# Attention by pairs of heads: both heads' output matmuls of a query quarter in one slot of the 20

## The chip, the cores and the metric

The kernel runs on one core of one Trainium2 chip. The metric is the device time of one execution in microseconds (us), and lower is better. Engine names are those of the profile: PE is the tensor engine's matmuls and PEld its weight loads, DVE is VectorE, ACT is ScalarE, POOL is GpSimd, and SP issues DMAs.

## The reference, cut to what matters

The network has three stages: a state-space convolution block, an attention block, and a mixture of eight experts. Only the attention is touched by the change.

```python
# x: (8, 128, 32, 32) float32 -> t: 8 images of 1024 tokens, 128 channels, 8 heads of 128
t = t + attn(ln(t))          # attention, below
t = t + experts(ln(t))       # router, top 2 of 8, gated experts

keys, queries, values = (einsum('btd,hod->bhto', x, W.reshape(8, 128, 128)) for W in (Wk, Wq, Wv))
dot  = einsum('bhqe,bhke->bhqk', queries, keys) / sqrt(128)
attn = softmax(where(causal, dot, -inf))
out  = einsum('bhqk,bhke->bqhe', attn, values).reshape(8, 1024, 1024)
return out @ Wu.T + bu
```

## The kernel before, in words

The attention takes the images in order and, in each, the eight heads as four **pairs**. There are 32 pairs `g`, four to an image (`g % 4` is 0 for an image's first pair and 3 for its last). The queries of a pair are cut into four **quarters** of 256 queries, and both heads of a quarter stand side by side in one matmul of 512 columns. A pair is worked off in 20 **slots**. The slot number `T` counts through all pairs, and `p = T % 20` is the slot within the pair. A slot handles one piece: the scores of one block of 128 keys against one quarter.

Each engine walks over the same slots `T` in its own instruction queue, in a fixed order written out in its loop, and waits on semaphores.

- **PE** issues, in slot `T`: three matmuls of `scores(T)` into one of three rotating PSUM banks, then the side work of the slot, then three matmuls of `attend(T - 3)` (the weighted sum, which needs the exponentials of three slots ago). `LAG = 3` is that distance. Scores and attend are done as three products of high and low halves (`mm3`, lines 1272 to 1274).
- **ACT** takes two exponentials of each piece (line 1439 writes `pf`, line 1441 the rounded `phi`), and copies the query projections (line 1454) and the finished sum of a quarter `u_sb` (line 1446).
- **POOL** subtracts the two for the low half `plo` (line 1213). In the first and the last pair of an image it also issues an indirect DMA (line 1232) in some slots.
- **DVE** adds the causal mask to the diagonal pieces (line 1603, `p` = 0, 1, 3, 5, 7, 10, 13, 17), finds the row maxima of the coming pair (`find_peaks`, lines 1585 and 1589), joins the maxima of two key halves (line 1598, slots 7 and 19; both of its inputs and its output are in SBUF), makes the low half of a query projection (`low_query`, line 1569) and adds the finished outputs (`add_output`: a reciprocal, line 1612, and two fused multiply-adds, line 1616).

**Side work and its banks.** All side work of PE goes through three PSUM banks, 3, 6 and 7. `side_uses(T)` lists the uses of a slot in order: `peaks` (every slot, for the piece 12 slots ahead, line 1327), in some slots of an image's last pair `tokens`, `queries` at `p` = 5, 7, 11 and 17 (for the next pair), `out`, in some slots the router's transposes and matmuls, and in an image's last pair transposed weights of an expert at `p` = 1, 3 and 15. The bank of a use is simply the next in the rotation, and `side_bank` makes PE wait until the consumer of the use three before has finished:

```python
def side_bank(signal, count):
    k = uses[0] % 3
    uses[0] += 1
    if side_free[k]:
        pe.wait_ge(side_free[k][0], side_free[k][1])
    side_free[k] = (signal, count)
    return side[k]
```

The bank of a `queries` use is free when `low_query` has read it (`q_ready`), that of an `out` when `add_output` has (`out_added`), that of a `peaks` when `find_peaks` has (`peak_found`), and that of the expert's `w1` or `w3` when `low_weights` has (line 1663).

**The outputs.** For each pair, quarter and head, `output` multiplies the sums of the quarter with the head's combined value-and-output matrix. It makes two matmuls in float32 of 129 columns (line 1361; the trace has four matmul records for them), into one side bank. `add_output` on DVE divides by the denominator and adds to `t_all`. Before the change each slot holds the output of one head: quarter 0 in slots 8 and 10, quarter 1 in 12 and 14, quarter 2 in 16 and 18, and quarter 3 in slots 4 and 6 of the next pair.

## Time and profile before

| | us |
|---|---|
| median of 3 runs (lowest to highest) | 2391.88 (2390.79 to 2393.61) |
| the profiled execution | 2386.38 |
| span of the profile, first to last instruction | 2384.3 |
| PE busy in the span | 2152.6 (90%) |
| DVE busy | 1700.9 (71%) |
| POOL busy | 1612.8 (68%) |
| ACT busy | 1251.6 (52%) |

The span is what the traced instructions cover, and the profiled execution's own time is 2.1 us longer. The first attention pair's scores begin some 780 us into the span and the attention is over by about 2020 us. What comes before is the convolution block, and what comes after is the experts and the last transposes. A full pair takes 35.6 us where it has no routing work beside it, and up to 39.4 us where it has.

### The profile page before, as it was taken

The page shows a single profiled execution, that of the slowest core. Times are in us where ns is not written, and L with a number is a line of the kernel's source. Part 1 is how long each engine was busy: PE and PEld are TensorE (multiplying, and loading weights), DVE is VectorE, ACT ScalarE, POOL GpSimd, SP SyncE. Part 2 cuts the span into 40 slices and gives each one's busy share as a digit, 9 for nine tenths or more (in the row PEclk, how much of TensorE's full clock was granted, in tenths as well). Part 3 has the DMA queues.
Part 4 walks back from the last instruction along what each step waited for, and adds up shares of the span by engine and source line. Part 5 has one row for each costly group of instructions (what it writes and reads, how often), then busy time and mean ns, then how long its engine had stood idle before and what let it go on. Part 6 is the DMA issues. An engine that isn't in the chain of part 4 may idle for free. (4 is left out here: it accounts for less than half of the span.)

```text
span 2384.3 us, 39643 instructions
## 1 busy us (share of the span) xinstructions
PE 2152.6 (90%) x11651; PEld 1739.3 (73%) x11651; DVE 1700.9 (71%) x4304; ACT 1251.6 (52%) x2559; POOL 1612.8 (68%) x1646
## 2 busy tenths in 40 slices
PE   4798898989996999999999999999999994699994
PEld 2466666666674888888888888888888883588883
DVE  5788987888855777787777887778777783344444
ACT  3555554545541666666666666666666662233331
POOL 2689878878872566678586786867868765355551
PEclk9878877878786999999999999999999996799996
DMA  2940000000000001001010010100101001455555
GB/s 75 387 168 10 10 1 9 10 1 1 1 19 18 10 1 25 1 9 36 2 42 3 8 37 2 40 5 7 38 1 38 7 6 38 168 193 188 190 179 212
DMA packets 135400, 130.91 MB, mean 55 GB/s; under 512 B 82885, under 2 KB 101359, under 8 KB 135190
## 3 DMA queue, kind: packets, MB, share of 16 engines
q1 hardware_dynamic: 124950, 107.12, 14.7%
q0 software_dynamic: 9088, 17.07, 2.1%
q10 hardware_dynamic: 1152, 4.19, 0.4%
q8 instruction: 98, 1.61, 0.3%
q14 instruction: 112, 0.92, 0.1%
HBM read 64.78 MB, written 65.10 MB: 54 GB/s over the span
## 5 line engine op out<-in xcount | busy, mean ns | idle before, releaser
L1213 POOL TENSOR_TENSOR plo<-pf,phi 128x512 fp32r<-128x512 f32 (+1 forms) x640 | 751.0, 1185 | 340.5 <-ACT phi L1441 309.9
L1439 ACT ACTIVATE pf<-psum 128x512 f32<-128x512 f32 (+1 forms) x640 | 357.1, 558 | 412.9 <-PE psum L1274 303.2
L1441 ACT ACTIVATE phi<-psum 128x512 fp32r<-128x512 f32 (+1 forms) x640 | 355.6, 556 | 0.0
L1585 DVE CUSTOM_DVE_ANT_0 psum<-psum,ahead_wide 128x128 f32<-128x128 f32 (+3 forms) x512 | 247.0, 503 | 69.0 <-PE psum L1327 64.7
L1272 PE MATMUL psum<-phi,x_tok 128*128 128x512 f32 (+1 forms) x640 | 265.7, 415 | 5.7 <-POOL plo L1213 5.7
L1866 POOL DMA_INDIRECT chosen<-yg,xg x156 | 152.5, 978 | 153.2 <-DVE yg L1978 115.1
L1327 PE MATMUL psum<-xT,qT 128*128 128x512 f32 (+3 forms) x768 | 244.8, 347 | 4.3 <-DVE peak L1585 3.3
L1272 PE MATMUL psum<-qT,xT 128*128 128x512 f32 (+1 forms) x640 | 237.5, 371 | 2.0 <-ACT phi L1441 1.3
L1273 PE MATMUL psum<-plo,x_tok 128*128 128x512 f32 (+1 forms) x640 | 237.4, 371 | 0.0
L1274 PE MATMUL psum<-phi,x_tok 128*128 128x512 f32 (+1 forms) x640 | 237.2, 371 | 0.0
L1273 PE MATMUL psum<-qT,xT 128*128 128x512 f32 (+1 forms) x640 | 236.2, 369 | 0.0
L1274 PE MATMUL psum<-qT,xT 128*128 128x512 f32 (+1 forms) x640 | 236.1, 369 | 0.0
L876 DVE SCALAR_TENSOR_TENSOR acc<-pad,cw,acc 128x1088 f32<-128x1088 f32 x128 | 200.0, 1563 | 3.4
L1589 DVE TENSOR_REDUCE peak<-psum 128x1 f32<-128x512 f32 x256 | 174.9, 684 | 28.8 <-PE psum L1327 24.2
L1970 DVE TENSOR_TENSOR hT<-act,psum 128x512 f32<-128x512 f32 (+1 forms) x117 | 80.3, 686 | 156.0 <-ACT act L1945 135.5
L1945 ACT ACTIVATE act<-psum 128x512 f32<-128x512 f32 (+1 forms) x117 | 69.7, 596 | 196.5 <-PE psum L1879 185.8
L1327 PEld LDWEIGHTS psum<-xT,qT 128*128 128x128 f32 x768 | 144.7, 190 | 37.8 <-DVE peak L1585 5.0
L1616 DVE SCALAR_TENSOR_TENSOR t_all<-psum,rinv,t_all 128x128 f32<-128x128 f32 x512 | 156.1, 347 | 9.1
L1361 PE MATMUL psum<-vu_w,u_sb 128*128 128x129 f32 x1024 | 159.4, 278 | 0.8 <-ACT u_sb L1446 0.8
L1361 PEld LDWEIGHTS psum<-vu_w,u_sb 128*128 128x128 f32 x1024 | 149.1, 191 | 14.1 <-issue 1.2
L1232 POOL DMA_INDIRECT routed<-xsC,slot x128 | 126.0, 984 | 42.7 <-issue 24.8
L513 PEld LDWEIGHTS psum<-xdt,Ldec 128*128 128x128 f32 x1024 | 127.0, 202 | 29.2 <-issue 29.2
(288 smaller groups left out, 5308.0 us busy)
## 6 DMA issues: line engine op xcount, KB each, us to landing
wg<-turned_w SPq DMA_DIRECT2D x39, 874.0 KB
routed<-empty SPq DMA_DIRECT2D x1, 34056.0 KB, 95.6
xg<-routed SPq DMA_DIRECT2D x39, 264.0 KB
qT<-nmax SPq DMA_DIRECT2D x512, 0.5 KB
y<-chosen SPq DMA_DIRECT2D x8, 1024.0 KB, 10.2
turned_w<-wT SPq DMA_DIRECT2D x8, 874.0 KB, 4.4
x_in_sb<-in_x SPq DMA_DIRECT2D x8, 512.0 KB, 3.2
out<-o_st ACTq DMA_DIRECT2D x8, 512.0 KB, 5.6
```

The costliest lines, as they stand in the source:

```text
L876: ins = v.scalar_tensor_tensor(dst, win, cw[:, m, tap:tap + 1], dst, ALU.mult, ALU.add)
L1213: g_.tensor_tensor(plo[:, T % RP, 0:n], pf[:, T % RF, 0:n], phi[:, T % RP, 0:n].bitcast(F32), ALU.subtract).then_inc(a["low_ready"], 1)
L1272: t.matmul(out_, left[1], right[0], start=start, stop=False)
L1273: t.matmul(out_, left[0], right[1], start=False, stop=False)
L1274: return t.matmul(out_, left[0], right[0], start=False, stop=stop)
L1327: last = t.matmul(to[:, col:col + n], qT[:, q_buffer(g, quarter), 0, q0:q0 + P], xT[:, b % 2, 0, k0:k0 + n], start=True, stop=True)
L1361: last = t.matmul(to[:, j * (P + 1):(j + 1) * (P + 1)], u_sb[:, quarter % 2, q0:q0 + P], vu_w[:, h, :], start=True, stop=True)
L1439: s_.activation(pf[:, T % RF, 0:n], bank[T % RS][:, 0:n], ACT.Exp)
L1441: s_.activation(phi[:, T % RP, 0:n], bank[T % RS][:, 0:n], ACT.Exp).then_inc(a["high_ready"], 1)
L1585: last = v.tensor_tensor_reduce(out=source[:, col:col + n], in0=source[:, col:col + n], in1=ahead_wide[:, HALF - n:HALF], scale=1.0, scala ...
L1589: last = v.reduce_max(to, source[:, 0:n], AX)
L1616: last = v.scalar_tensor_tensor(tile, source[:, j, 0:P], rinv[:, n % 2, j:j + 1], tile, ALU.mult, ALU.add)
```

## The change

Both outputs of a quarter move into one slot. The slot is that of the first head of before, so the second head's output comes two slots sooner: from 10 to 8, 14 to 12, 18 to 16 and 6 to 4. PE's, DVE's and the bank rotation's orders follow. The peaks, the queries and all other side work keep their slots. Since the rotation is by order of use, the bank of nearly every later use changes, and with it the use that it has to wait for.

```diff
             QUERY_AT = {5: 0, 7: 1, 11: 2, 17: 3}
-            OUT_AT = {8: (0, 0), 10: (0, 1), 12: (1, 0), 14: (1, 1), 16: (2, 0), 18: (2, 1)}
-            OUT_LATE = {4: (3, 0), 6: (3, 1)}
+
+            OUT_AT = {8: 0, 12: 1, 16: 2}
+            OUT_LATE = {4: 3}
...
-                if p in OUT_LATE and is_pair(g - 1):
-                    yield "out", g - 1, *OUT_LATE[p]
-                if p in OUT_AT and is_pair(g):
-                    yield "out", g, *OUT_AT[p]
+                for hh in range(2):
+                    if p in OUT_LATE and is_pair(g - 1):
+                        yield "out", g - 1, OUT_LATE[p], hh
+                    if p in OUT_AT and is_pair(g):
+                        yield "out", g, OUT_AT[p], hh
...
-                        if p in OUT_LATE and is_pair(g - 1):
-                            add_output(g - 1, *OUT_LATE[p])
-                        if p in OUT_AT and is_pair(g):
-                            add_output(g, *OUT_AT[p])
+                        for hh in range(2):
+                            if p in OUT_LATE and is_pair(g - 1):
+                                add_output(g - 1, OUT_LATE[p], hh)
+                            if p in OUT_AT and is_pair(g):
+                                add_output(g, OUT_AT[p], hh)
```

## Rows read from the trace of the kernel before

**Rows 1.** The page, part 1: busy us, share of the span, instructions.

```profile
PE 2152.6 (90%) x11651; PEld 1739.3 (73%) x11651; DVE 1700.9 (71%) x4304; ACT 1251.6 (52%) x2559; POOL 1612.8 (68%) x1646
```

**Rows 2.** Busy time by stretch: start:end, length, engines, granted clock, DMA share, GB/s.

```profile
850.00:1850.00 1000.00, 988.09 (x5608) 850.88 (x5608) 784.15 (x2440) 656.10 (x1337) 723.67 (x634) 1.00 0.09 18
```

**Rows 3.** PE's waits from 850 to 1850 us: total us, times, longest.

```profile
PE psum L1272 <- DVE peak L1589: 5.7, 6, 1.0
```

**Rows 4.** Timeline of PE, slot 12 of pair 11: start, us, instruction, count.

```profile
1212.41 0.39 PE L1327 MATMUL psum<-xT,qT 128*128 128x512 f32 x1
1212.63 0.61 PE L1361 MATMUL psum<-vu_w,u_sb 128*128 128x129 f32 x4
1213.00 0.48 PE L1272 MATMUL psum<-phi,x_tok 128*128 128x512 f32 x1
1213.31 0.40 PE L1273 MATMUL psum<-plo,x_tok 128*128 128x512 f32 x1
```

**Rows 5.** Timeline of PE, slot 19 of pair 11, which has no output.

```profile
1226.24 0.40 PE L1327 MATMUL psum<-xT,qT 128*128 128x256 f32 x2
1226.47 0.40 PE L1272 MATMUL psum<-phi,x_tok 128*128 128x512 f32 x1
1226.71 0.40 PE L1273 MATMUL psum<-plo,x_tok 128*128 128x512 f32 x1
```

**Rows 6.** Timeline of PE, slot 8 of pair 10.

```profile
1167.09 0.33 PE L1327 MATMUL psum<-xT,qT 128*128 128x128 f32 x2
...
1167.88 0.28 PE L1273 MATMUL psum<-plo,x_tok 128*128 128x256 f32 x1
```

**Rows 7.** Timeline of DVE, slot 7 of pair 10.

```profile
1167.11 0.69 DVE L1569 TENSOR_TENSOR qT<-psum,qT 128x512 fp32r<-128x512 f32 x1 [0.84 <-ACT qT L1454]
```

**Rows 8.** The same two places in pair 0 and pair 30, PE and DVE.

```profile
794.31 0.33 PE L1327 MATMUL psum<-xT,qT 128*128 128x128 f32 x2
...
794.33 0.69 DVE L1569 TENSOR_TENSOR qT<-psum,qT 128x512 fp32r<-128x512 f32 x1 [0.84 <-ACT qT L1454]
...
1926.74 0.33 PE L1327 MATMUL psum<-xT,qT 128*128 128x128 f32 x2
...
1926.76 0.69 DVE L1569 TENSOR_TENSOR qT<-psum,qT 128x512 fp32r<-128x512 f32 x1 [0.84 <-ACT qT L1454]
```

**Rows 9.** Timeline of PE, slot 5 of pair 10 (an image's third pair).

```profile
1159.11 0.50 PE L1327 MATMUL psum<-xT,qT 128*128 128x512 f32 x1 [0.47 <-DVE peak L1585]
1160.56 0.39 PE L1272 MATMUL psum<-xT,qk_w 128*128 128x256 f32 x1 [0.95 <-DVE peak L1589]
1160.79 0.28 PE L1273 MATMUL psum<-xT,qk_w 128*128 128x256 f32 x1
1160.90 0.28 PE L1274 MATMUL psum<-xT,qk_w 128*128 128x256 f32 x1
```

**Rows 10.** Timeline of DVE, slots 4 and 5 of pair 10.

```profile
1159.83 0.68 DVE L1589 TENSOR_REDUCE peak<-psum 128x1 f32<-128x512 f32 x1
1160.62 0.61 DVE L1616 SCALAR_TENSOR_TENSOR t_all<-psum,rinv,t_all 128x128 f32<-128x128 f32 x2
1161.14 0.42 DVE L1603 TENSOR_TENSOR psum<-psum,mask_after 128x256 f32<-128x256 f32 x1
```

**Rows 11.** Timeline of PE and DVE, slots 3 and 4 of pair 11 (an image's last).

```profile
1195.95 0.39 PE L1327 MATMUL psum<-xT,qT 128*128 128x512 f32 x1
...
1196.52 0.51 DVE L1663 TENSOR_TENSOR wT<-psum,wT 128x341 fp32r<-128x341 f32 x1 [1.03 <-ACT wT L1481]
```

**Rows 12.** Timeline of ACT, POOL, DVE, slots 7 and 8 of pair 11.

```profile
1203.15 0.59 ACT L1441 ACTIVATE phi<-psum 128x512 fp32r<-128x512 f32 x1
...
1202.86 1.31 POOL L1213 TENSOR_TENSOR plo<-pf,phi 128x512 fp32r<-128x512 f32 x1
...
1204.11 1.29 POOL L1213 TENSOR_TENSOR plo<-pf,phi 128x512 fp32r<-128x512 f32 x1
...
1203.26 2.17 DVE L1598 TENSOR_TENSOR nmax<-peak 128x4 fp32r<-128x4 f32 x1
```

## The prediction

> **What bounds the kernel now.** I read the page first: PE is busy for 90% of the span and no other engine for more than 71% [rows 1]. An average over stages says little, so I took the stretches next. Between 850 and 1850 us, where only attention runs, PE is busy for 988.1 of 1000 us at a granted clock of 1.00, while DVE has 784 and POOL 724 [rows 2]. PE's own list of waits there is short, and its largest entry is 5.7 us behind `find_peaks` [rows 3]. So the attention is bound by PE's queue. Work taken from PE or a wait put into it moves the end one for one, and spare time on DVE is worth nothing unless PE waits for DVE. All that PE idles in that stretch is 11.9 us, which bounds what any relief of waits alone can give: about 12 to 14 us over the whole attention.
>
> The last view was the timeline of single slots. For each use of a side bank I wrote down when PE would reach it and when the use three before is released. That is the whole question of this change.
>
> **The work of PE is unchanged.** There are 256 outputs of four matmul records each before and after. A first look suggests that an output also costs a switch. Behind it the first attend matmul keeps the next away for 0.31 us (1213.00 to 1213.31), and without one for 0.24 us (1226.47 to 1226.71) [rows 4, 5]. Half of the 256 switches would go, about 0.08 us each, some 10.8 us with the finer times of the records. I don't take this. From the start of the peaks to the second attend matmul it is 0.90 us with an output (1212.41 to 1213.31) and 0.47 us without (1226.24 to 1226.71) [rows 4, 5]. The difference of 0.43 to 0.44 us is four records at 0.11 us. The first three stand 0.11 us apart as well, since four records and the short step behind them fill 0.37 us (1212.63 to 1213.00) [rows 4]. The record of the first attend matmul starts early by just what the interval after it has too much. So I price two outputs in a row at 0.88 us, twice one, and the saving at 0. The other bound is 0.08 us for each of 128 joins, 10.8 us, a rival below.
>
> **The new waits, one by one.** In order of use the banks' rule gives, for slots 4 to 8: `queries` of slot 5 waits for the first output of slot 4 (before: for the peaks of slot 4), the peaks of slot 6 for the second output, and the second output of slot 8 for `low_query` of slot 7 (before: the peaks of slot 9 did, more than 1 us later). The second outputs of 12 and 16 wait for slot 11's `low_query` and slot 15's last use, and in an image's last pair the second output of slot 4 waits for `low_weights` of slot 3.
>
> *Slot 8, all pairs but the last.* In pair 10 the peaks start at 1167.09 and the second attend matmul at 1167.88, 0.79 us later [rows 6]. A matmul of 256 columns takes 0.12 us here (1160.79 to 1160.90) [rows 9], so PE is free for the next thing 0.67 us after the peaks, at 1167.76. The second output would start there. Its bank is free at the end of `low_query`, 1167.11 + 0.69 = 1167.80 [rows 7]. After a release PE starts 0.05 us later: `find_peaks` ends at 1160.51 and the waiting matmul starts at 1160.56 [rows 9, 10]. And the first matmul behind a wait keeps the next away for 0.23 instead of 0.12 us [rows 9], 0.11 us more, as its weights were not loaded ahead. Lateness 0.04 + 0.05 + 0.11 gives 0.20 us. The sum could lose 0.06 if the refill is shorter, and with no refill at all it is 0.09; it could not be below nothing. The Trainium skill, in TensorE: Matmul & The Clock Gate, section LDWEIGHTS, gives a weight load of P columns about P/1.2 ns, so 107 ns for 128. By that page's figure these waits carry 3.3 us of refill in all; the row's 0.11 us agrees.
>
> This lateness isn't an accident of one pair. `low_query` hangs on a chain that starts with slot 7's scores on PE itself (mask, two exponentials, query copy, `low_query`), and DVE sits idle for 0.84 us before it, waiting for ACT [rows 7]. In pair 0 and in pair 30 it starts 0.02 us after the peaks of slot 8, as in pair 10 [rows 6 to 8]. I found the same within 0.02 us in 24 of the 31 pairs that have this step. Clearing DVE's slot 6 doesn't help, since ACT, not DVE, is last. 31 pairs by 0.20 us: **6.3 us**.
>
> *Slot 5 of an image's third pair.* Here DVE is behind with the router's work and PE already waits. Slot 5's peaks start at 1159.11 and its queries at 1160.56, when `find_peaks` of slot 4 is done [rows 9, 10]. After the change the peaks of slot 5 wait for that same `find_peaks`, and the queries behind them for the first output's addition, which ends at 1160.62 + 0.61 = 1161.23 [rows 10]. So queries start at 1161.28 or 1161.29, 0.73 us later. Of this 0.44 us is the second output that now lies before them and is gone from slot 6. Left is 0.29 us in seven images: **2.0 us**. If PE also had to wait for the second addition, another 0.71 us of DVE (1160.43 to 1161.14), it would be 5 us more, but that bank is the peaks' of slot 6, which come 2 us later.
>
> *Slot 4 of an image's last pair.* The second output waits for `low_weights`, which ends at 1196.52 + 0.51 = 1197.03. PE would reach it at 1195.95 + 0.67 = 1196.62 [rows 11]. With 0.05 and 0.11 that is 0.57 us. Against it go two waits that PE now has in this pair, about 0.23 us behind the queries of slot 5 and about 0.36 us in slot 9, both on banks that will be freed long before. Sum: nothing, or 0.1 us to either side in each of seven pairs.
>
> *Slot 7 of the last pair.* The join on DVE took 2.17 us here against 0.16 us elsewhere, as it stood through two of POOL's subtractions, 1202.86 to 1204.17 and 1204.11 to 1205.40 [rows 12]. `low_query` follows and ends at 1206.03. This is what frees the bank for slot 8's second output. The 0.34 us that this pair is now late (0.57 less 0.23) moves `phi` of slot 7 from 1203.74 to 1204.08. POOL's second subtraction could then start about 1204.16, where back to back it started at 1204.11, and the join may slip in between. If it does, the pair pays only the usual 0.20 us. If it doesn't, PE stands from 1205.16 to 1206.08, 0.92 us, 0.72 more. In one of the seven pairs by the records POOL has half a microsecond in hand and the long join stays for certain: **0.7 us**. For the other six it is open, 0 or 4.3 us. By the Trainium skill (SBUF — State Buffer, section Who interferes with whom) a DVE instruction with two SBUF inputs and a GpSimd instruction that reads SBUF block each other for the whole instruction, by order of issue. The 2.17 us row agrees, and the rule leaves open who wins a gap of 0.05 us.
>
> *The rest at nothing.* Slot 12's second output has about 0.26 us in hand after refill, as `low_query` of slot 11 is 0.42 us ahead. Slot 16's comes more than 1 us after the peaks of 15 are found. The masks of slots 13 and 17 move later by 0.7 us of DVE, but DVE waited there for PE, which is itself 0.44 us later. Slot 5's mask comes some 0.3 us late against PE; behind it on DVE are `find_peaks` and `low_query`, whose bank is wanted about 1 us later, in slot 7. If this cover were gone it would be 0.3 us a pair, 9 us. Between an image's first and second pair DVE is behind with normalising, and the addition gone from slot 18 makes it 0.3 us earlier, which slot 4's second addition takes back: 0, at most 2 us either way.
>
> **Sum.** 6.3 + 2.0 + 0.7 = 9.0 us. The profiled execution would go from 2386.38 to 2395.4. It was 5.5 us below the median, which has no part in the sum; on the median of 2391.88 the forecast is **2400.9**, 0.38% slower.
>
> **Rivals.**
> - *The long join stays in all seven images.* 9.0 + 4.3 gives 2405.2. For it: POOL took the port back to back each time. Against it: the lateness of 0.34 us is just above POOL's margin.
> - *The switch costs what it seems to.* Place: behind each output in PE's queue, at 0.08 us for 128 joins. 9.0 - 10.8 gives 2390.1, no change. From 0.108 us a join it outweighs the waits by more than 0.2%, and the kernel is faster, 2387 and below; had the waits in slot 8 no cost besides, 2384 or less. For it is the interval of 0.31 us, against it the sum over the slot [rows 4, 5].
> - *Nothing binds.* The wait in slot 8 rests on 0.2 us. If `low_query` comes 0.16 us sooner than its chain now does, or the refill is hidden behind the matmuls in flight, only 2.7 us remain: 2394.6, no change that could be measured. Against it stands that the same offset shows from pair 0 to pair 30 [rows 8].
>
> **Chances.** Forecast 0.43, long join 0.27, switch cost 0.16 (half of it beyond the point where it decides), nothing binds 0.14. The measurement tells about 0.2% (4.8 us) from no change. So slower 0.70, no change 0.22 (0.14 and 0.08), faster 0.08. The range for 8 in 10 goes from the switch rival's 2390 to 2408, a little over the long join, for the 2 us left open between images. The forecast's own range is 2397 to 2404: the slot 8 wait between 0.14 and 0.25 us, and the 2 us.
>
> **What would show it.** Right: PE's list of waits has a new entry, the output (line 1361, as matmul or weight load) waiting for DVE line 1569, about 31 times. The eight records of two outputs and the step into attend take as long as twice 0.44 us. In third pairs the queries of slot 5 wait for line 1616. Seven pairs or fewer have joins over 2 us. Pairs without routing go from 35.65 to 35.85 us. Wrong: if the switch were real, those pairs would get shorter by 0.34 us before any wait. If `low_query` were no longer last, no wait of line 1361 would show. A join of 2 us in pairs that now have 0.16 us, or the granted clock below 1.00 inside the attention, would be a cause that I don't have.

## The result, and the profile after

The changed kernel takes 2412.11 us (median of six runs, 2404.80 to 2418.04) where the kernel before takes 2388.07 us (six runs, 2380.35 to 2393.61). The ratio is 1.0103, 95% interval 1.0072 to 1.0134: slower by 24 us, where the forecast said 9. The sign was right and the time lies outside the range.

The page's first part and the stretch from 850 to 1850 us, of the changed kernel. Attention lines stand two lower than before (1361 is now 1363).

```profile
PE 2170.9 (90%) x11651; PEld 1749.4 (72%) x11651; DVE 1719.5 (71%) x4304; ACT 1245.3 (52%) x2559; POOL 1613.8 (67%) x1646
...
850.00:1850.00 1000.00, 976.38 (x5487) 836.83 (x5487) 782.26 (x2401) 634.86 (x1304) 704.41 (x615) 1.00 0.08 16
```

As in [rows 1] the instructions are the same in number. PE now idles for 23.6 us of this stretch, where it idled for 11.9 us [rows 2], and the clock is 1.00 in both. The 11.7 us more of idle time are only part of the loss: the same stretch holds 5487 matmul records in place of 5608, 2.2% fewer, which is some 22 us' worth (an estimate). The rest of the lost time counts as busy, as slot 8 below shows. PE's waits in the same stretch (total us, times, longest):

```profile
PE psum L1363 <- DVE peak L1587: 7.0, 6, 1.2
PE psum L1329 <- DVE peak L1587: 6.5, 6, 1.3
PE psum L1274 <- ACT phi L1443: 2.6, 5, 0.5
...
PE psum L1363 <- DVE qT L1571: 0.9, 1, 0.9
```

The entry that should be there 31 times, the output (1363) behind `low_query` (1571), stands there once, for its one long wait. The largest entries are six waits each. Six of a kind in 1000 us means one in each image, so the next view is the time of each pair, from its first scores matmul to the next pair's. The differences to before, in us, worked out from those starts in the timelines of PE:

| pairs | each pair | sum | forecast, by its own terms |
|---|---|---|---|
| an image's first (8) | 0.17, 0.21, then 0.32 to 0.40 | 2.6 | 1.6 |
| second (8) | 0.15, 0.79, then 1.04 to 1.08 | 7.3 | 1.6 |
| third (8) | 0.15, then 2.15 to 2.23, but 0.91 in pair 14 and 0.71 in pair 30 | 12.7 | 3.6 |
| last (7) | 0.47, 0.84, then 0.09 to 0.13 | 1.9 | 2.1 |
| all | | 24.5 | 9.0 (8.9 in these rounded terms) |

The span grew by 29.9 us in the two profiled executions. Of that 5.2 us lie ahead of the attention's first scores (780.17 against 785.33 us), in code that did not change. That start varies between 769 and 789 us over the kernels of this study, and the mean granted clock of the stretch ahead of it goes with it: 0.83 where it took 769.2 us (experiment 4), 0.81 in the kernel before, 0.78 where it took 788.8 us (experiment 1). So from here on kernels are compared by their pair times, which repeat within some hundredths.

**Slot 8**, pair 10, PE and DVE, and slot 16 of the same pair:

```profile
1178.96 0.33 PE L1329 MATMUL psum<-xT,qT 128*128 128x128 f32 x2
1179.13 1.31 PE L1363 MATMUL psum<-vu_w,u_sb 128*128 128x129 f32 x8
1180.19 0.36 PE L1274 MATMUL psum<-phi,x_tok 128*128 128x256 f32 x1
...
1178.98 0.69 DVE L1571 TENSOR_TENSOR qT<-psum,qT 128x512 fp32r<-128x512 f32 x1 [0.84 <-ACT qT L1456]
...
1193.89 1.11 PE L1363 MATMUL psum<-vu_w,u_sb 128*128 128x129 f32 x8
1194.75 0.48 PE L1274 MATMUL psum<-phi,x_tok 128*128 128x512 f32 x1
```

This is as forecast. `low_query` starts 0.02 us after the peaks, as in [rows 6, 7], and from the first output to attend it takes 1.06 us, against 0.86 us in slot 16 where nothing is waited for: 0.20 us. The eight records show it as 1.31 us busy against 1.11, with no idle time between them, so no list of waits has it. And two outputs in a row take 0.86 us, so there is no sign of 0.08 us saved on the 0.88 us.

**Slots 4 and 5**, pair 10, PE and DVE:

```profile
1170.67 0.71 PE L1363 MATMUL psum<-vu_w,u_sb 128*128 128x129 f32 x4 [1.18 <-DVE peak L1587]
...
1172.84 0.39 PE L1274 MATMUL psum<-xT,qk_w 128*128 128x256 f32 x1 [0.22 <-DVE t_all L1618]
...
1170.00 0.56 DVE L1587 CUSTOM_DVE_ANT_0 psum<-psum,ahead_wide 128x384 f32<-128x384 f32 x1
```

Against [rows 9]: the waits of 0.47 and 0.95 us in slot 5 are gone, and 1.18 us stand before the second output in slot 4, which waits for `find_peaks` of slot 3, and 0.22 us before the queries. I had placed the wait elsewhere, but the net is the one forecast (experiment 2).

**Slots 16 and 17**, pair 10, PE, DVE and POOL. Here is what I did not have:

```profile
1197.07 0.50 PE L1329 MATMUL psum<-xT,qT 128*128 128x512 f32 x1 [1.04 <-DVE peak L1587]
...
1193.17 0.81 DVE L1560 CAST xT<-xT_all 128x512 fp32r<-128x512 f32 x1
1193.89 1.24 DVE L1721 CAST slot<-slot_f 128x16 int32<-128x16 f32 x1
...
1195.34 1.04 DVE L1723 TENSOR_TENSOR before<-before,fresh 128x8 bf16<-128x8 bf16 x1
1196.41 0.30 DVE L1587 CUSTOM_DVE_ANT_0 psum<-psum,ahead_wide 128x128 f32<-128x128 f32 x1
...
1191.14 5.22 POOL L1215 TENSOR_TENSOR plo<-pf,phi 128x512 fp32r<-128x512 f32 x4 [1.74 <-ACT phi L1443]
```

PE waits for `find_peaks` of slot 16. That is late because three of DVE's instructions ahead of it took 0.81, 1.24 and 1.04 us while POOL subtracted four times without a pause. In the kernel before they took 0.42, 0.17 and 0.95 us.

**Slot 7 of a last pair**, pair 11, DVE and POOL, against [rows 12]:

```profile
1217.41 0.64 DVE L1600 TENSOR_TENSOR nmax<-peak 128x4 fp32r<-128x4 f32 x1
...
1216.71 2.54 POOL L1215 TENSOR_TENSOR plo<-pf,phi 128x512 fp32r<-128x512 f32 x2
```

The join slips in between POOL's two subtractions: 0.64 us in place of 2.17 us. Six last pairs had the long join before, pairs 7 to 27. In five of them it is now 0.60 to 0.64 us. In pair 7 it takes 2.06 us, and PE waits 0.90 us behind it.

**Slots 16 and 19 of a first pair**, pair 8 (scores at 1085.67), POOL and PE:

```profile
1119.57 1.28 POOL L1215 TENSOR_TENSOR plo<-pf,phi 128x512 fp32r<-128x512 f32 x1
...
1120.90 0.50 PE L1274 MATMUL psum<-phi,x_tok 128*128 128x512 f32 x1
1121.24 0.40 PE L1275 MATMUL psum<-plo,x_tok 128*128 128x512 f32 x1
```

POOL's subtraction for slot 16 ends at 1120.85, and attend in slot 19, which needs it, starts 0.05 us later and keeps the next matmul away for 0.34 us, where it is 0.23 us in the kernel before. This is a wait too short for the list, like the one in slot 8. Up to slot 19 the pair is 0.21 us late and behind it 0.40. In the kernel before POOL had 1.2 us in hand here, and now it comes 1.4 us later in the pair.

### The profile page after: what moved, and what is told of

It reads as the page before. It is cut to its first block and busy times, and to the rows that moved or that the text cites. A ratio compares the mean times of both kernels' runs of the same rounds, so it can differ in the third digit from the quotient of the medians.

```text
span 2414.2 us, 39643 instructions
## 1 busy us (share of the span) xinstructions
PE 2170.9 (90%) x11651; PEld 1749.4 (72%) x11651; DVE 1719.5 (71%) x4304; ACT 1245.3 (52%) x2559; POOL 1613.8 (67%) x1646
## 5 line engine op out<-in xcount | busy, mean ns | idle before, releaser
L1274 PE MATMUL psum<-phi,x_tok 128*128 128x512 f32 (+1 forms) x640 | 255.8, 400 | 5.6 <-POOL plo L1215 5.6
L1276 PE MATMUL psum<-phi,x_tok 128*128 128x512 f32 (+1 forms) x640 | 236.8, 370 | 0.0
L1363 PE MATMUL psum<-vu_w,u_sb 128*128 128x129 f32 x1024 | 149.5, 284 | 12.0 <-DVE peak L1587 8.2
L1363 PEld LDWEIGHTS psum<-vu_w,u_sb 128*128 128x128 f32 x1024 | 133.7, 192 | 24.5 <-DVE peak L1587 9.6
```

Of the source, the lines that this page charges most:

```text
L1274: t.matmul(out_, left[1], right[0], start=start, stop=False)
L1276: return t.matmul(out_, left[0], right[0], start=False, stop=stop)
L1363: last = t.matmul(to[:, j * (P + 1):(j + 1) * (P + 1)], u_sb[:, quarter % 2, q0:q0 + P], vu_w[:, h, :], start=True, stop=True)
```

## The experiments

In all of these kernels a table entry is a list, and PE and DVE run through it, so that each quarter can be put in one slot or two. Their lines are those of the kernel before. Experiments 1 to 8 and 12 are one execution each, so their verdict is their pair times.

### 1. Only quarter 0 in one slot (slot 8)

```diff
-            OUT_AT = {8: (0, 0), 10: (0, 1), 12: (1, 0), 14: (1, 1), 16: (2, 0), 18: (2, 1)}
+            OUT_AT = {8: [(0, 0), (0, 1)], 12: [(1, 0)], 14: [(1, 1)], 16: [(2, 0)], 18: [(2, 1)]}
```

> Quarter 0 alone has both outputs in slot 8; the other three quarters stand as before. Two theories of the 24 us. Banks: each second output waits in PE's queue for a use of its bank that ends late, so every quarter costs what its own wait costs. Here that is the wait for low_query of slot 7, 0.15 us in each of 31 pairs, 4.6 us in all, the same in all four pairs of an image (35.65 to 35.80 us where there is no routing), and the second and third pairs keep the rest of their times of before. DVE: the two additions in a row put DVE late where it is already behind, whatever bank they use. Then the first pairs stay at 35.65 us and the second and third pairs take 0.3 us more or over. If a switch of matmul kind were saved, the first pairs would be below 35.65 us.

2410.56 us (before beside it: 2392.14). First pairs +0.19 us each (pair 0 +1.76), second +0.21 to 0.53, third +0.13 to 0.25, last +0.20 in pair 3 and then +0.81 to 0.85. Sum 13.3 us. In pair 0, 1.56 of the 1.76 us are not the change's. They arise in slots 3 to 5, and slot 4 ran at the lower level of the clock, where the kernel before has a granted clock of 1.00 (start:end, length, engines, granted clock, DMA share, GB/s):

```profile
795.19:797.54 2.35, 2.35 (x8) 1.95 (x7) 0.40 (x1) 1.10 (x3) 2.15 (x2) 0.50 0.74 214
```

Without them it is 11.7 us, about half of what the whole change costs. The wait in slot 8 is what was forecast. The second pairs lose another 0.27 us at their very start, with a new wait of PE of 0.20 to 0.23 us for `find_peaks` at the peaks of slot 0. So each theory holds in part. The last pairs show what the other case of the join looks like; pair 11, DVE and PE:

```profile
1216.49 2.19 DVE L1598 TENSOR_TENSOR nmax<-peak 128x4 fp32r<-128x4 f32 x1
...
1219.34 0.71 PE L1361 MATMUL psum<-vu_w,u_sb 128*128 128x129 f32 x4 [1.03 <-DVE qT L1569]
```

Without the outputs of quarter 3 in slot 4, nothing in this pair is late, the join stays at 2.16 us or more, and the pair pays 0.83 us. The forecast priced a pair with a long join at 0.20 + 0.72 us, and took it that this depends on 0.34 us of lateness from slot 4. Both hold.

### 2. Only quarter 3 in one slot (slot 4 of the next pair)

```diff
-            OUT_LATE = {4: (3, 0), 6: (3, 1)}
+            OUT_LATE = {4: [(3, 0), (3, 1)]}
```

> Quarter 3 alone has both outputs in slot 4 of the next pair. Banks: in an image's third pair the second output waits for find_peaks of slot 3, about 1.2 us, and the waits of slot 5 that the kernel before has (0.5 and 0.95 us in the trace) shrink to 0.2 us: 0.7 to 1.2 us more in each of seven third pairs, 5 to 8 us in all; last pairs within 0.2 us; first pairs at 35.65 us. DVE: the same sum, but the second pairs too, where DVE is behind in slots 0 to 4, by 0.3 us or more. I expect 7 us in all.

2396.69 us (before 2392.14). Third pairs +0.25 to 0.32 us (forecast 0.29), second +0.21 to 0.28 (forecast 0, at most 2 us in all: 1.75), first 0, last about -0.14 except +0.26 in pair 3. Sum 3.2 us, half of the 7 us expected, and the join is short in five last pairs as in the changed kernel. In slots 4 and 5 of pair 10 PE waits for 1.19 us before the second output and 0.23 us before the queries, in place of 0.47 and 0.95 us [rows 9]. The idle time is the same, 1.42 us, and the pair still pays what was forecast. A cost of waits is not only their idle time.

### 3. Only quarter 2 in one slot (slot 16)

```diff
-            OUT_AT = {8: (0, 0), 10: (0, 1), 12: (1, 0), 14: (1, 1), 16: (2, 0), 18: (2, 1)}
+            OUT_AT = {8: [(0, 0)], 10: [(0, 1)], 12: [(1, 0)], 14: [(1, 1)], 16: [(2, 0), (2, 1)]}
```

> Quarter 2 alone has both outputs in slot 16. Banks: in third pairs the peaks of slot 17 now wait for those of 16, which DVE finds late behind the router's counts of slot 15: 1.0 us in each of seven, and nothing in first, second and last pairs. DVE: the second addition, in slot 16 in place of 18, also delays the mask and the normalising of slot 17 in first pairs, which the second pair pays for in slots 0 to 3, 0.5 us or more in each of seven. I expect both, 10 to 12 us in all.

2391.04 us (before 2392.14). First pairs -0.01 us each, second -0.16 and then -0.29 to -0.39, third +0.10 to 0.23, last about 0. Sum -1.4 us, where 10 to 12 us were expected: neither theory's cost is there. The first pairs are the cleanest test of the rival that a join saves PE a switch: each has one join here and nothing waits. They gain 0.01 us, where the rival said 0.08. The gain in the second pairs is the addition that is gone from slot 18, where DVE is behind.

### 4. The whole change, with the second addition's own wait moved

The second addition's reciprocal waits until the addition before it has landed. Here it waits one addition less, and the wait stands behind it.

```diff
-                        need2(dve, "out_added", n)
+                        need2(dve, "out_added", n - 1)
...
-                        dve.wait_ge(a["rinv_ready"], n + 1)
+                        dve.wait_ge(a["rinv_ready"], n + 1); need2(dve, "out_added", n)
```

> The changed kernel, but the wait of an addition for the one before it stands behind the reciprocal and not ahead of it. In the changed kernel's trace the second addition starts 0.10 us of idle after the first, and its reciprocal behind that; before, other work lay between. Each second addition should end 0.1 to 0.2 us sooner. Banks: where PE waits for find_peaks or low_query this changes nothing, so the third pairs keep their times and the first pairs 35.8 us at the start; 0 to 2 us in all. DVE: second and third pairs get back 0.2 us a piece or more, 3 to 6 us in all.

2398.45 us (before 2392.14), but its attention starts at 769.2 us, 16 us sooner than the changed kernel's, in unchanged code. By pairs it stands at 23.1 us against 24.5: first pairs +0.16 to 0.23 in place of 0.32 to 0.40, and the others as in the changed kernel. So 0.18 us in six first pairs hang on the length of the second addition: POOL's subtraction for slot 16 ends 0.23 us sooner in the pair, and attend in slot 19 no longer waits for it. The 15 us that are sought do not.

### 5. Only quarter 1 in one slot (slot 12)

```diff
-            OUT_AT = {8: (0, 0), 10: (0, 1), 12: (1, 0), 14: (1, 1), 16: (2, 0), 18: (2, 1)}
+            OUT_AT = {8: [(0, 0)], 10: [(0, 1)], 12: [(1, 0), (1, 1)], 16: [(2, 0)], 18: [(2, 1)]}
```

> Quarter 1 alone has both outputs in slot 12. In the changed kernel's third pairs the cast of the router's slots on DVE took 1.24 us in place of 0.17, one slot after slot 14, from which the addition is gone, and PE stood 1.04 us for the peaks of slot 16. Quarters 0, 2 and 3 alone did not bring this back. Theory port: without the addition in slot 14 DVE comes to these SBUF-only instructions sooner, while POOL subtracts, and blocks on it; then this kernel shows the 1.24 us cast and 1 us or more in each of seven third pairs, 7 to 9 us in all, nothing in first pairs. Theory combination: the loss needs several quarters at once (a second addition in slot 16 as well, since that puts find_peaks of slot 16 under PE's next use of the bank); then the cast may be long here but PE hardly waits, under 2 us in all.

2397.38 us (before 2384.21). First pairs -0.02 us, second +0.45 and then +0.94 to 0.99, third +1.46 to 1.57 (0.23 in pair 14, 0.10 in pair 30), last 0. Sum 14.0 us, for the quarter that the forecast had put at nothing. Of the two theories only theory port fits, with 7.9 us in third pairs, and neither had the 6.2 us of the second pairs. The loss has two places.

*Between first and second pair.* Pair 8 of the kernel before (scores at 1075.57), DVE, POOL, DVE:

```profile
1098.98 0.61 DVE L1616 SCALAR_TENSOR_TENSOR t_all<-psum,rinv,t_all 128x128 f32<-128x128 f32 x2
1099.50 0.42 DVE L1603 TENSOR_TENSOR psum<-psum,mask_after 128x256 f32<-128x256 f32 x1
...
1101.17 1.29 POOL L1213 TENSOR_TENSOR plo<-pf,phi 128x512 fp32r<-128x512 f32 x1 [0.98 <-ACT phi L1441]
...
1106.12 0.20 POOL L1220 TENSOR_TENSOR rsb<-mvb,epst 128x8 f32<-128x8 f32 x1
...
1108.45 2.92 DVE L1656 TENSOR_SCALAR xsC<-t_all,mvb,rsb 128x128 f32<-128x128 f32 x3
1111.29 0.68 DVE L1589 TENSOR_REDUCE peak<-psum 128x1 f32<-128x512 f32 x1
```

And with quarter 1 in slot 12 (scores at 1072.75), DVE, POOL, DVE, PE:

```profile
1097.09 0.61 DVE L1616 SCALAR_TENSOR_TENSOR t_all<-psum,rinv,t_all 128x128 f32<-128x128 f32 x2
1097.62 0.42 DVE L1603 TENSOR_TENSOR psum<-psum,mask_after 128x256 f32<-128x256 f32 x1
...
1099.28 1.29 POOL L1213 TENSOR_TENSOR plo<-pf,phi 128x512 fp32r<-128x512 f32 x1 [1.90 <-PE psum L1274]
...
1104.23 0.21 POOL L1220 TENSOR_TENSOR rsb<-mvb,epst 128x8 f32<-128x8 f32 x1
...
1106.23 3.27 DVE L1656 TENSOR_SCALAR xsC<-t_all,mvb,rsb 128x128 f32<-128x128 f32 x3 [0.54 <-POOL rsb L1222]
1109.42 0.68 DVE L1589 TENSOR_REDUCE peak<-psum 128x1 f32<-128x512 f32 x1
...
1110.15 0.50 PE L1327 MATMUL psum<-xT,qT 128*128 128x512 f32 x1 [0.92 <-DVE peak L1589]
```

Less the start of the pair: the mask of slot 13 goes from 23.93 to 24.87 us, POOL's subtraction for that slot from 25.60 to 26.53, POOL's deviations (1220) from 30.55 to 31.48, the normalising (1656) from 32.88 to 33.48, `find_peaks` behind it from 35.72 to 36.67, and PE waits 0.92 us at the peaks of slot 0. In neither kernel does the mask wait for PE: there is no bracket on its row. DVE comes to it late, behind the four statistics of line 1636, and the second addition makes it 0.93 us later at once. From there to the deviations POOL works on with a pause of 0.15 us in both kernels, and so nothing takes the 0.93 us back.

*Slot 17 of third pairs.* The kernel before, pair 10 (scores at 1150.66), DVE and POOL:

```profile
1181.12 0.42 DVE L1558 CAST xT<-xT_all 128x512 fp32r<-128x512 f32 x1
1181.45 0.17 DVE L1719 CAST slot<-slot_f 128x16 int32<-128x16 f32 x1
...
1178.62 2.54 POOL L1213 TENSOR_TENSOR plo<-pf,phi 128x512 fp32r<-128x512 f32 x2 [1.27 <-ACT phi L1441]
1181.44 1.31 POOL L1213 TENSOR_TENSOR plo<-pf,phi 128x512 fp32r<-128x512 f32 x1 [0.28 <-ACT phi L1441]
```

With quarter 1 in slot 12, pair 10 (scores at 1148.78), DVE, POOL and PE:

```profile
1179.24 0.80 DVE L1558 CAST xT<-xT_all 128x512 fp32r<-128x512 f32 x1
1179.96 1.25 DVE L1719 CAST slot<-slot_f 128x16 int32<-128x16 f32 x1
...
1177.22 5.22 POOL L1213 TENSOR_TENSOR plo<-pf,phi 128x512 fp32r<-128x512 f32 x4 [1.74 <-ACT phi L1441]
...
1183.16 0.39 PE L1272 MATMUL psum<-xT,qk_w 128*128 128x256 f32 x1 [1.25 <-DVE peak L1585]
```

POOL's run of subtractions starts 0.48 us later in the pair (28.44 against 27.96 us), and so it goes on without the pause of 0.28 us (before 1181.44) that DVE's cast of `xT` and the slot cast right behind it met before. The slot cast waits: 1.25 us in place of 0.17, the cast of `xT` 0.80 in place of 0.42, and `find_peaks` of slot 16 comes 1.55 us later (33.71 against 32.16 us). DVE comes to the cast of `xT` at the same time in the pair in both kernels, 30.46 us. It is POOL that has moved, and not DVE that comes sooner, as I had expected.

The trace of before had this already, once. The slot cast in it, and PE's wait:

```profile
L1719 DVE CAST slot<-slot_f x8: 164/168/1255, 1029.7 to 2010.8; 128x16 int32<-128x16 f32 x8
...
PE psum L1272 <- DVE peak L1585: 1.3, 1, 1.3
```

The cast of 1255 ns is that of pair 14, which took 39.58 us before, where pairs 6 and 10 took 38.08 and 38.02 us. The changed kernel adds 0.91 us there in place of 2.2, since the collision had been paid. In pair 30, which adds 0.71 us, the cast takes 0.55 us.

### 6. The whole change, with the router's counts in slot 18

```diff
-                        if (place_, p) == (2, 15):
+                        if (place_, p) == (2, 18):
```

> The changed kernel with the router's counts (the cast, the sum over both and the running sum) in slot 18 in place of 15. If the third pairs' wait in slot 17 (1.04 us for the peaks and 0.17 us for the queries) comes from these instructions, it is gone and each of seven third pairs takes 1.0 to 1.3 us less than in the changed kernel, 38.0 + 1.0 us or so; 7 to 9 us in all. If it comes from the double addition or the bank alone, it stays.

2405.53 us (before 2384.21). Third pairs +0.40 to 0.46 us (pair 14: -1.07) in place of 2.15 to 2.23, and all others as in the changed kernel. Sum 13.4 us against 24.5: one reordering on DVE takes back 11 us. The slot cast is at 0.16 us in all images, and PE's six waits in front of the peaks (line 1329 in the changed kernel, 1327 here) are gone. The 0.42 us that are left are close to the forecast's own two terms for these pairs, 0.20 + 0.29.

### 7. All quarters but quarter 2 in one slot each

```diff
+            OUT_AT = {8: [(0, 0), (0, 1)], 12: [(1, 0), (1, 1)], 16: [(2, 0)], 18: [(2, 1)]}
+            OUT_LATE = {4: [(3, 0), (3, 1)]}
```

> The changed kernel with quarter 2 back in slots 16 and 18. Slot 17's peaks then wait for the peaks of 15, as before. Theory bank: the wait in slot 17 needs the double use in slot 16, so it is gone whatever the cast takes: third pairs 1.0 to 1.3 us less than in the changed kernel. Theory port: DVE is late by the same 1 us and PE waits elsewhere, the third pairs lose less than 0.4 us of their excess. In second pairs the 0.5 us wait of slot 3 should go too if the double addition in slot 16 makes it, and stay if it is slot 18's missing addition.

2418.56 us (before 2384.21); sum 26.1 us: first and last pairs as in the changed kernel, second +1.46 to 1.51 in place of 1.05, third +1.94 to 2.02 in place of 2.2. So theory bank fails: without the double use in slot 16 the third pairs still pay 2.0 us. Joining quarter 2 adds only 0.2 us there, and gives 0.4 us back in a second pair, both as in experiment 3. In second pairs PE waits for 0.96 us at the peaks of slot 0, as in experiment 5, and the wait for ACT in slot 3 that the changed kernel has is gone.

### 8. The other way: one output a slot, two slots later

```diff
+            OUT_AT = {10: [(0, 0)], 12: [(0, 1)], 14: [(1, 0)], 16: [(1, 1)], 18: [(2, 0)], 19: [(2, 1)]}
+            OUT_LATE = {6: [(3, 0)], 8: [(3, 1)]}
```

> The kernel before with its eight outputs, one to a slot, but two slots later: quarter 3 in slots 6 and 8 of the next pair, then 10, 12, 14, 16, 18 and 19. PE has no output in slots 4 and 5, where third pairs wait for DVE with the router's work. Banks: the peaks and queries of slot 5 then wait for uses one further back, and most of the 0.47 and 0.95 us waits of third pairs go, up to 1.9 us in each of seven, 8 to 13 us less than before. DVE: DVE itself is the bound there, the waits move to the masks and scores of slots 5 to 8, and less than 0.6 us a pair is gained. First pairs stay at 35.65 us.

2379.27 us (before 2384.21). Second pairs -1.03 to -1.09 us, third -0.85 to -1.27, last 0, but first pairs +2.22 to 2.26, where the output of slot 19 waits 1.3 us for `find_peaks` behind the normalising. Sum +0.8 us, where 8 to 13 us less were hoped for: the 4.9 us that the single execution is faster are not in the pairs, and it reached the attention 9 us sooner, at 771.1 us. The third pairs gain in slot 5, where PE's waits of 0.47 and 0.95 us have become one of 0.41 us. The second pairs gain in slots 0 to 3, right behind the wait that the first pair has paid, and the two together are 1.2 us longer.

### 9. The second addition one slot later on DVE

PE as in the changed kernel; DVE makes each second addition in the next slot, behind that slot's `find_peaks` and `low_query`. The line for `OUT_LATE` is changed in the same way.

```diff
-                        for x_ in (OUT_AT.get(p, ()) if is_pair(g) else ()):
+                        for x_ in (OUT_AT.get(p, [])[:1] + OUT_AT.get(p - 1, [])[1:] if is_pair(g) else ()):
                             add_output(g, *x_)
```

> The changed kernel's order on PE and in the banks, but DVE adds each second head's output one slot later, behind that slot's mask and peaks. Theory mask: what costs is not the output's bank but that DVE does the second addition ahead of the mask of slot 13 (and 5 and 17). The mask is 0.9 us late, POOL's subtraction with it, and POOL then stands on the port when DVE normalises (second pairs lose 0.95 us with quarter 1 alone) and when it casts the router's slots (third pairs lose 1.5). Then first to last pairs return to the kernel before plus slot 8's wait of 0.15 to 0.2 us and slot 4's 0.3 us in third pairs: 6 to 9 us in all over 30 pairs in place of 24.5. Theory load: DVE has the same work in the same stretch, and second and third pairs keep most of their 1.05 and 2.2 us.

2532.39 us (four runs, 2529.24 to 2534.86), ratio to before 1.0603, interval 1.0565 to 1.0642. Its largest wait of PE from 850 to 1850 us:

```profile
PE psum L1327 <- DVE t_all L1616: 67.7, 74, 1.9
```

It loses 144 us where the changed kernel loses 24. The second output's bank is the peaks' of two slots on, and PE reaches it before DVE is through. An addition put off behind the next slot's peaks and `low_query` comes too late for three banks, and the run says nothing on theory mask.

### 10. One output a slot, quarter 2 where it was, counts in slot 18

```diff
+            OUT_AT = {10: [(0, 0)], 12: [(0, 1)], 14: [(1, 0)], 15: [(1, 1)], 16: [(2, 0)], 18: [(2, 1)]}
+            OUT_LATE = {6: [(3, 0)], 8: [(3, 1)]}
...
+                        if (place_, p) == (2, 18):
```

> A version that should beat both: one output to a slot, quarter 3 in slots 6 and 8 of the next pair, then 10, 12, 14, 15, 16 and 18, and the router's counts in slot 18 in place of 15. Slots 4 and 5 have no output and the first pairs keep their order in 16 and 18. Banks: third pairs lose their waits in slot 5 as in the run with all outputs later, 0.9 us less in each of seven, and the one pair with a 1.25 us wait in slot 17 loses that: 7 to 8 us less than before in the attention, 0.3%. Theory mask: the addition in slot 15 and the one in 14 put nothing ahead of the masks of 13 and 17 that was not there, so second pairs stay within 0.2 us; if they lose 0.5 us or more, the chain from mask to POOL to port is met again, and nothing is gained.

2381.49 us (12 runs, 2376.18 to 2390.91) against 2388.09 us (17 runs, 2377.41 to 2397.15), ratio 0.9979, interval 0.9959 to 0.9999. Of the kernels run more than once this has the lowest median, 0.2% under the kernel before by the ratio, and the interval ends just short of 1. The attention gives only 1.3 us of it, no more than experiment 3's 1.4: third pairs -0.51 to -0.60 (pairs 14 and 30 -2.11 and -0.91), second -0.38 to -0.42, but first +0.63 and last +0.54. Its PE waits:

```profile
PE psum L1272 <- DVE peak L1585: 4.2, 6, 0.7
PE psum L1327 <- DVE qT L1569: 3.5, 6, 0.6
```

One is a new wait for `low_query` in slot 9 of last pairs. The other is what is left of the waits of third pairs in slot 5. The 7 to 8 us that I had hoped for from this schedule were not there. Most of the rest of the 6.6 us between the medians goes with the clock of the executions. Eight of these 12 runs had a mean granted clock of 0.917 to 0.919, and of the 17 runs of the kernel before two had, at 2377.41 and 2378.13 us. At 0.911 this kernel took 2390.4 to 2390.9 us and the kernel before 2392.3 and 2393.4.

### 11. The whole change, second addition right behind the next slot's mask

```diff
+                        for x_ in (OUT_AT.get(p - 1, [])[1:] if is_pair(g) else ()):
+                            add_output(g, *x_)
...
-                        for x_ in (OUT_AT.get(p, ()) if is_pair(g) else ()):
+                        for x_ in (OUT_AT.get(p, [])[:1] if is_pair(g) else ()):
                             add_output(g, *x_)
```

> The changed kernel's order on PE and in the banks, but DVE does each second addition at the start of the next slot, right behind its mask and ahead of find_peaks and low_query. The run before this one put it behind low_query, and the peaks two slots on then waited 0.9 us for its bank in every pair; this avoids that. Theory mask: with the mask no longer behind the second addition POOL is late only by PE's own 0.44 us, and the long casts and most of the 1.05 and 2.2 us of second and third pairs go: 7 to 12 us over 30 pairs in place of 24.5. Theory load: only what lies between two masks counts, DVE has the same work, and 18 us or more stay.

2412.70 us (four runs, 2409.23 to 2419.54), ratio to before 1.0111, interval 1.0079 to 1.0143: no better than the changed kernel, and not the 7 to 12 us of theory mask. Second pairs +0.50 to 0.53 us in place of 1.05: half of their loss hung on the second addition ahead of the mask. Third pairs +2.88 to 2.98 in place of 2.2. Sum 27.3 us, 25.7 without the 1.56 us of pair 0, where the granted clock of slot 4 was 0.50 as in experiment 1.

### 12. Only quarter 1 in one slot, second addition right behind the mask of slot 13

```diff
+            OUT_AT = {8: [(0, 0)], 10: [(0, 1)], 12: [(1, 0), (1, 1)], 16: [(2, 0)], 18: [(2, 1)]}
...
+                        for x_ in (OUT_AT.get(p - 1, [])[1:] if is_pair(g) else ()):
+                            add_output(g, *x_)
```

> Quarter 1 alone in slot 12 (14.0 us over 30 pairs in its own run: 0.95 us in second pairs, 1.5 us in third pairs, first pairs unchanged), with its second addition behind the mask of slot 13. Theory mask: the mask of slot 13 comes 0.45 us later than before in place of 0.93, POOL with it; if that is early enough for POOL to be done before DVE casts and normalises, both losses fall under 0.3 us and the sum under 4 us. Theory load or an offset of any size is enough: second and third pairs keep at least half, 7 us or more.

2405.60 us (before 2387.75, median of seven). Second pairs +0.48 to 0.59 us in place of 0.95, with PE's wait at the peaks of slot 0 at 0.45 us in place of 0.92. Third pairs +2.15 to 2.29 in place of 1.5, but 3.55 in pair 30, of which 1.6 us arise in slots 5 and 6 at a granted clock of 0.86 and 0.65. Sum 18.7 us, 17.1 without them, against 14.0 with the addition ahead of the mask: under 4 us had been hoped for, and it is no gain. In pair 8 (scores at 1078.73) the mask of slot 13 starts at 24.38 us in the pair, 0.45 us later than before, and now waits for PE:

```profile
1103.11 0.43 DVE L1603 TENSOR_TENSOR psum<-psum,mask_after 128x256 f32<-128x256 f32 x1 [0.35 <-PE psum L1274]
```

So of the 0.93 us in experiment 5 half is the addition, and the half that is left is PE's second output, 0.44 us, ahead of the scores of slot 13. Pair 10 (scores at 1154.30), DVE and POOL:

```profile
1181.05 0.43 DVE L1603 TENSOR_TENSOR psum<-psum,mask_after 128x256 f32<-128x256 f32 x1 [0.86 <-PE psum L1274]
...
1183.00 1.10 DVE L1714 TENSOR_TENSOR picked<-first,spot 128x64 f32<-128x64 f32 x1
1184.03 1.33 DVE L1715 TENSOR_TENSOR picked<-second,spot 128x64 f32<-128x64 f32 x1
...
1182.73 3.77 POOL L1213 TENSOR_TENSOR plo<-pf,phi 128x512 fp32r<-128x512 f32 x3 [1.74 <-ACT phi L1441]
```

Here the mask waits for PE, and it starts at 26.75 us in the pair, the same as with the addition ahead of it (26.76), against 26.28 before. So in third pairs the 0.48 us are not DVE's: they are the second output on PE, 0.44 us, ahead of the scores of slot 13. POOL's run follows them. DVE comes to the two products 0.71 us later than in experiment 5, as the addition now lies between the mask and them, and so they fall into POOL's run: they take 1.10 and 1.33 us, where they took 0.23 and 0.22.

## Why the prediction was wrong in size

**The bound: right.** PE's queue sets the end. The work of PE is the same, and the pairs take 24.5 us more, with the medians 24.0 us apart.

**No saving on a switch: right.** First pairs with one join and no wait change by -0.01 us (experiment 3) and -0.02 us (experiment 5), where the interval of [rows 4] suggested 0.08.

**The wait in slot 8: right.** Forecast 0.20 us a pair; 0.15 to 0.17 us in pairs 0 to 2, 0.19 us in the first pairs of experiment 1.

**Slot 5 of third pairs: right in size, wrong in place.** Forecast 0.29 us, measured 0.25 to 0.32 (experiment 2). PE waits in slot 4 before the second output, not in slot 5. I had looked up the banks of `queries` and `peaks` there, and not followed who holds the bank of slot 4's second output in a third pair.

**The last pairs: right in sum.** The join became short in five of the six pairs that had it long, as taken, and pair 7 paid 0.84 us. Experiment 1 shows the other case at 0.83 us a pair, against 0.92 taken. The forecast counted seven long joins where the kernel before has six: pair 3's is short, so the rival of the long join was 3.6 and not 4.3 us dearer. Sum 1.9 against 2.1 us.

**The rest at nothing: this step failed.** It said that the masks of slots 13 and 17 "move later by 0.7 us of DVE, but DVE waited there for PE, which is itself 0.44 us later". I had spoken for all pairs with one sentence. For the mask of slot 13 both halves of the sentence break, each in its own pairs.

- In an image's *first* pair DVE does not wait there for PE. The mask has no idle time before it, so all of the second addition, with its reciprocal and the gap ahead of it 0.91 and not 0.7 us, goes through. By way of the exponentials, POOL's queue and the normalising it reaches PE as 0.92 us at the start of the second pair (experiment 5), and moving only the addition halves it (experiments 11 and 12). Forecast 0; alone it cost 6.2 us in the second pairs, which in the whole change stand 5.7 us over their forecast. The half that is left when the addition is moved is PE's own 0.44 us. In the whole change the loss shows in another row, a wait in slot 3 of 0.50 to 0.54 us for ACT's `phi` in pairs 9 to 29, since the addition gone from slot 18 relieves slot 0 (experiments 3 and 7). By slot 3 these pairs are then 0.57 us late, and not 0.97.
- In an image's *third* pair DVE does wait for PE, and PE's own 0.44 us, which I counted as cover, are the harm. They move POOL's run of subtractions onto DVE instructions that work in SBUF alone. Moving three of those away takes 11.1 us back (experiment 6). Forecast 3.6 us for these pairs, measured 12.7.

I had read one such collision, the join's [rows 12], and priced it for that one instruction. The list of slow instructions of the same kind in the trace of before would have named the others: the cast with 168 ns in the middle and 1255 at the longest, in a pair 1.5 us longer than its like. By the Trainium skill (SBUF — State Buffer, section Who interferes with whom) DVE instructions in a two-port mode, or with two SBUF inputs, and GpSimd's share one pair of ports, held by whoever issues first for its whole instruction. The rows agree on which instructions suffer: what grows here are casts and products between SBUF tiles, while `find_peaks`, which reads PSUM, takes 0.30 us in both kernels.

The effects do not add up. Quarters 0 to 3 alone cost 11.7 (without the clock's part in pair 0), 14.0, -1.4 and 3.2 us, 27.5 in all, against 24.5 together. Most of the difference is the long join: the last pairs pay 5.2 us with quarter 0 alone and 1.9 us with all four. The first pairs' 0.18 us beyond the wait in slot 8 are the wait for POOL in slot 19. In experiment 11, with the mask of slot 13 ahead of the second addition, they are gone, so this too is the lateness that the forecast took to be covered. *Open* stays why the granted clock fell just there in pair 0 of experiments 1 and 11 and in pair 30 of experiment 12, and why the third pairs of experiment 2 are 0.29 us longer with the same idle time.

## What to carry to other kernels

When an edit is costed at nothing because "the engine waited there anyway", check the row of that instruction in every kind of stage the loop runs through, not in one: here the idle bracket was there in some pairs and not in others. A few tenths of a microsecond of shift on the bounding engine are not cover but a cause, if another engine's run follows it: look for instructions of DVE between SBUF tiles whose shortest and longest duration differ several times over, because here those marked where the next shift would hurt. And where a whole execution varies by half a per cent in code that isn't touched, compare stage by stage within the traces, and look at the granted clock of each stage before a difference is put down to the change.

## What the runs showed of the hardware

- A DVE cast of 128x16 between SBUF tiles took 0.17 us, and 1.24 us when POOL subtracted without a pause beside it. Products of 128x64 went from 0.23 to 1.10 and from 0.22 to 1.33 us, and a cast of 128x512 from 0.42 to 1.32 us.
- Between two subtractions of POOL in a row either engine can win: the join of 128x4 stood for 2.06 to 2.19 us through the rest of one subtraction and the whole of the next, and for 0.64 us where it slipped in between. The first product of experiment 12 slipped in as well (1.10 us), and the second stood through a whole subtraction (1.33 us). What decides it these runs don't show.
- Two accumulations of four records in a row, in two banks, take 0.86 us, as long as two apart. A wait ahead of the second costs its own time and about 0.1 us more: in slot 8 the bank was free some 0.1 us after PE could have used it, and attend came 0.20 us later.
- The attention's start, after some 780 us of unchanged code, lay between 769 and 789 us in single executions, at mean granted clocks from 0.83 to 0.78, while the pair times repeated within some hundredths. Two runs of the kernel before took 2377.41 us at 0.919 and 2397.15 us at 0.909.
- At a granted clock of 0.50 a slot of pair 0 took 2.35 us (experiment 1), where it took 1.27 us at 1.00.
